# Filler products taken out of a four-layer fused transformer kernel

## The chip, the cores and the metric

The kernel runs on one core of one Trainium2 chip. The metric is the device time of one execution in microseconds (us), lower is better; where several executions of one program are shown, the median stands for them.

The core has four engines with a queue of their own: PE (TensorE, matrix products), DVE (VectorE), ACT (ScalarE) and POOL (GpSimd). SP issues transfers. The profile also prints the clock that PE was granted: 1.00 is its upper level of 2.4 GHz, 0.50 its lower one of 1.2 GHz.

## The reference

Eight sublayers work one after the other on `x` (2048 tokens of 128 numbers) with a context of the same shape. Each takes the layer norm of `x` and adds its gated output to `x`. Cut to what matters:

```python
x = x + tanh(g_xattn[0]) * _L0_xattn_ref(_layernorm(x), ctx, ctx)
x = x + tanh(g_ffn[0])   * _L0_ffn_ref(_layernorm(x), ...)        # turn 0: 16 experts, top 2, and a shared one
x = x + tanh(g_xattn[1]) * _L1_xattn_ref(_layernorm(x), ctx, ...) # turn 1: 16 heads
x = x + tanh(g_ffn[1])   * _L1_ffn_ref(_layernorm(x), ...)        # turn 2: 8 experts, normed twice
x = x + tanh(g_xattn[2]) * _L2_xattn_ref(_layernorm(x), ctx, ctx, mask, ...)  # turn 3
x = x + tanh(g_ffn[2])   * _L2_ffn_ref(_layernorm(x), ...)        # turn 4: 4 experts, top 2
x = x + tanh(g_xattn[3]) * _L3_xattn_ref(ctx, _layernorm(x), ...) # turn 5
x = x + tanh(g_ffn[3])   * _L3_ffn_ref(_layernorm(x), ...)        # turns 6 and 7: attention, then 8 experts

def _L1_ffn_ref(x, Wr, br, W1, b1, g1, be1, W2, b2, g2, be2):
    p = softmax(xt @ Wr + br); probs, idx = top_k(p, 2); probs = probs / probs.sum(-1)
    h = _layernorm(relu(einsum('td,edf->etf', xt, W1) + b1), g1, be1)
    y = _layernorm(relu(einsum('etf,efd->etd', h, W2) + b2), g2, be2)
    return einsum('te,etd->td', gate, y)
```

## The kernel before

The 2048 tokens are worked through in four passes (`for i in range(BLOCKS)`) of 512 tokens, each held as four tiles of 128 tokens. All weights stay on the chip. A pass goes through eight stages in a fixed order; a stage turns its normed rows (tokens by features) into columns with products against the unit matrix, and the code numbers these places 0 to 7: "turn 2" starts the doubly normed experts (`ffn1`), turn 3 the masked attention behind it (`attention` with `k_x2`), turn 4 the four experts `ffn2`, turn 7 the eight experts `ffn3`. Everything is written out by hand: the order on each engine is the order of the code, the four passes are unrolled, and semaphores connect the engines. All data are f32, and a product of 128x512 shows in the profile as two MATMUL records with a weight load (PEld) before each.

At a turn PE has to wait: the last rows of the stage before must be added to `x` (DVE), normed (`layer_norm`, DVE with a root taken by POOL, `give_root`, L251) and then turned (`turn_pairs`, L342, or `turn_pair`, L348) in two pairs of tiles; ACT copies the turned pair to `xnT` (L358, L353), and the first products of the stage follow.

The function `keep_clock` (L331) issues n products of the unit matrix with a weight matrix into bank 1. Nobody reads them. In each pass there are 12:

- in the tail of `ffn1`, two behind the transposes of the combination table (L1045, the call is at L1047), ahead of the wait for ACT's copy of that table, and two behind the product with that table (L1050, the call at L1052), ahead of the wait for the last expert's rows `y` (DVE L1171 to L1177), which the last product L1054 adds;
- by `FILL_BEFORE_ROWS` two at turn 3 (before L348), three at turn 4 and three at turn 7 (before L342), each ahead of the wait for the normed rows `rows_ready`.

After L1054, DVE adds the sum to `x` (L1201) and norms it for turn 3. There, PE computes the queries (L534), the mask products (L479) and the scores (L487). At turn 4 the router products (L1234) let DVE choose the experts (L1301 to L1313), and the products L1243 with the relus L1283 on ACT follow. At turn 7 it is the router L1784, then the products L1792 with the gelus L1850.

```python
FILL_BEFORE_ROWS = (0, 0, 0, 2, 3, 0, 0, 3)
```

Of the kernel before, what the change touches and what calls it, by code (L numbers as in the profile page):

```python
# [34 lines left out]
L3F = dict(wr=8, n1=D, n2=D, w1=8 * 256, w2=16 * D)  # L35


FILL_BEFORE_ROWS = (0, 0, 0, 2, 3, 0, 0, 3)


def width(pieces):
    return sum(pieces.values())
# [63 lines left out]
def wait_for(engine, signal):  # L106
    sem, value = signal
    engine.wait_ge(sem, value)
# [31 lines left out]
def build(nc, args, out):  # L140
    ctx = ExitStack()
    with ctx:
        def sb(name, shape, dt=F32):
            return ctx.enter_context(nc.sbuf_tensor(name, shape, dt))
# [5 lines left out]
        w_x1 = sb("w_x1", [P, width(XA) + width(XB)])  # L150
# [47 lines left out]
        banks = [ctx.enter_context(nc.psum_tensor(f"bank{i}", [P, 512], F32)) for i in range(8)]  # L198
# [10 lines left out]
        ident = k_const["ident"]  # L209
# [70 lines left out]
        def pair_tiles(pair):  # L280
            return (2 * pair, 2 * pair + 1)
# [42 lines left out]
            link(dve.scalar_tensor_tensor(x[:, :, :], rows, tg[:, 7:8], x[:, :, :], ALU.mult, ALU.add))  # L324
            dve.sem_inc(rows_ready, 2)

        def keep_clock(pe, bank, n):


            for _ in range(n):  # L330
                pe.matmul(bank[:, :], ident, w_x1[:, 0:512], start=True, stop=True)  # L331

        def turn_pairs(pe, prev, turn, rows):

            if prev is not None:
                wait_for(pe, prev.bank0)
            for pair in range(2):
                if pair == 0:
                    keep_clock(pe, banks[1], FILL_BEFORE_ROWS[turn])
                pe.wait_ge(rows_ready, 2 * turn + pair + 1)  # L340
                for t in pair_tiles(pair):
                    m = pe.transpose(banks[pair][:, (t % 2) * P:(t % 2 + 1) * P], rows[:, t, :], ident)  # L342
                m.then_inc(rows_turned, 1)

        def turn_pair(pe, turn, rows, pair, bank):
            pe.wait_ge(rows_ready, 2 * turn + pair + 1)
            for t in pair_tiles(pair):
                m = pe.transpose(bank[:, (t % 2) * P:(t % 2 + 1) * P], rows[:, t, :], ident)  # L348
            m.then_inc(rows_turned, 1)
# [99 lines left out]
        def attention(prev, turn_no, after, w, kv, kv_waits, q_bias, neg, finish):  # L449
# [14 lines left out]
            def body(block, q_done, q_ready, scored,  # L464
# [8 lines left out]
                def _(pe):  # L473
# [62 lines left out]
                    if not here:  # L536
                        for signal in kv_waits:
                            wait_for(pe, signal)
                    wait_for(pe, prev.bank0)
                    keep_clock(pe, banks[1], FILL_BEFORE_ROWS[turn_no])  # L540
                    turn_pair(pe, turn_no, xn, 0, banks[0])
                    if kv is kv1:
                        pe.wait_ge(weights_loaded, 16 * 4)
# [238 lines left out]
        def ffn0(i, prev, turn_no, after):  # L782
# [15 lines left out]
            def body(block, rest_cleared, routed, halves_ready, sig_ready, comb_ready, up_done, sil_ready, weighted, hid_ready,  # L798
# [4 lines left out]
                @block.tensor  # L803
                def _(pe):
                    turn_pairs(pe, prev, turn_no, xn_next)
                    pe.wait_ge(l0_loaded, 16)
                    pe.wait_ge(rowsT_ready, 2 * turn_no + 2)
# [151 lines left out]
        def ffn1(prev, turn_no, after):  # L959
# [19 lines left out]
            def body(block, x_done, routed, half_ready, sig_ready, up_done, hT_ready, squares_summed, squared, down_done,  # L979
                     first_variance, first_root, y_raw, second_variance, second_root, y_ready, added, coef_ready,  # L980
                     combT_done, combT_ready, last_done):
                def z_of(e, t):
                    return banks[4 + 2 * (e % 2) + t // 2][:, (t % 2) * 130:(t % 2) * 130 + 130]

                @block.tensor
                def _(pe):
                    kv2.keys(pe, banks[2])
                    kv2.values(pe, 0, banks[4])
                    kv2.values(pe, 1, banks[5])
                    turn_pairs(pe, prev, turn_no, xn)  # L990
                    wait_for(pe, prev.all_used)
                    pe.wait_ge(rowsT_ready, 2 * turn_no + 2)
                    for t in range(TILES):
                        m = pe.matmul(banks[3][:, t * 8:(t + 1) * 8], xnT[:, t * P:(t + 1) * P], k_f1["wr"],
                                      start=True, stop=True)
                    m.then_inc(routed, 1)

                    def up(e):
                        for c in range(4):
                            n = 4 * e + c  # L1000
                            if n >= 3:
                                pe.wait_ge(hT_ready, n - 2)
                            if n == 2:
                                pe.wait_ge(kv2.k_ready, 1)
                            pe.matmul(banks[n % 3][:, :], k_f1["w1"][:, e * 512 + c * P:e * 512 + (c + 1) * P], xnT[:, :],  # L1005
                                      start=True, stop=True).then_inc(up_done, 1)

                    def down(e):
                        pe.wait_ge(hT_ready, 4 * e + 4)
                        if e >= 2:  # L1010
                            pe.wait_ge(y_raw, e - 1)
                        if e == 0:
                            pe.wait_ge(kv2.v_ready, TILES)
                        for t in range(TILES):
                            for c in range(4):
                                pe.matmul(z_of(e, t)[:, 0:129], hT[e % 2][:, c, t * P:(t + 1) * P], w_f1d[:, c, e, :],  # L1016
                                          start=(c == 0), stop=(c == 3))

                    def sum_squares(e):
                        pe.wait_ge(squares_summed, e + 1)  # L1020
                        for t in range(TILES):
                            m = pe.matmul(z_of(e, t)[:, 129:130], sq[e % 2][:, 0, t * P:(t + 1) * P], ones[:, 0:1],
                                          start=True, stop=True)
                        m.then_inc(down_done, 1)

                    def add(e):
                        pe.wait_ge(y_ready, e + 1)
                        if e == 0:
                            pe.wait_ge(half_ready, 1)
                        pe.matmul(banks[3][:, :], ident, y[e % 2].rearrange("p t d -> p (t d)"), start=(e == 0),  # L1030
                                  stop=False).then_inc(added, 1)

                    up(0)
                    for e in range(EXPERTS):
                        if e + 1 < EXPERTS:
                            up(e + 1)
                        down(e)
                        sum_squares(e)
                        if e >= 1:
                            add(e - 1)  # L1040

                    pe.wait_ge(hT_ready, 4 * EXPERTS)
                    pe.wait_ge(coef_ready, 1)
                    for t in range(TILES):
                        m = pe.transpose(banks[0][0:16, t * P:(t + 1) * P], stack[:, t, :], ident)  # L1045
                    m.then_inc(combT_done, 1)
                    keep_clock(pe, banks[1], 2)  # L1047
                    pe.wait_ge(combT_ready, 1)
                    for t in range(TILES):
                        pe.matmul(banks[3][:, t * D:(t + 1) * D], combT[:, t * P:(t + 1) * P], w_f1b[:, :],  # L1050
                                  start=False, stop=False)
                    keep_clock(pe, banks[1], 2)  # L1052
                    pe.wait_ge(y_ready, EXPERTS)
                    pe.matmul(banks[3][:, :], ident, y[(EXPERTS - 1) % 2].rearrange("p t d -> p (t d)"), start=False,  # L1054
                              stop=True).then_inc(last_done, 1)
# [158 lines left out]
        def ffn2(prev, turn_no, after):  # L1214
# [11 lines left out]
            def body(block, routed, shifted, exp_ready, comb_ready, up_done, r_ready,  # L1226
                     sum_ready, turned, gT_ready, down_done, taken):
                @block.tensor
                def _(pe):
                    turn_pairs(pe, prev, turn_no, xn)  # L1230
                    wait_for(pe, prev.all_used)
                    pe.wait_ge(rowsT_ready, 2 * turn_no + 2)
# [936 lines left out]
```

## Time and profile before

| | us |
|---|---|
| median of 3 executions (1696.64 to 1699.97) | 1697.77 |
| the profiled execution | 1694.08 |
| its span, first to last instruction | 1692.3 |
| PE busy in it | 1421.5 (84%) |
| DVE busy | 1087.9 (64%) |
| ACT busy | 736.3 (44%) |
| POOL busy | 410.0 (24%) |
| mean granted clock of PE | 0.939 |

The profile is one execution. Every row of a timeline says when a run of equal instructions began, how long it took, on which engine and line, and in brackets how long the engine had been idle before it and what ended the wait. A row over a stretch of time gives the busy time of each engine in it and the clock that PE was granted there.

### The profile page before, as it was taken

How to read it: one execution, taken by the hardware profiler on the slowest of the kernel's cores; microseconds unless marked ns; L12 is line 12 of the kernel's file. 1: busy time of each engine (PE TensorE's matmuls, PEld its weight loads, DVE VectorE, ACT ScalarE, POOL GpSimd, SP SyncE). 2: the span in 40 equal slices, each digit the busy share in tenths (PEclk: the TensorE clock that was granted, in tenths of full speed). 3: DMA queues.
4: the chain of work that ended last, by engine and by line, in shares of the span. 5: the costliest groups of instructions: out<-in, count | busy, mean ns of one | idle time of the engine just before them, and what ended most of it. 6: DMA issues, size and time to landing. Idle time of an engine off the chain costs nothing. (4 is left out here: it accounts for less than half of the span.)

```text
span 1692.3 us, 28855 instructions
## 1 busy us (share of the span) xinstructions
PE 1421.5 (84%) x11038; PEld 930.3 (55%) x11038; DVE 1087.9 (64%) x3306; ACT 736.3 (44%) x1397; POOL 410.0 (24%) x318
## 2 busy tenths in 40 slices
PE   5788988897877988798878898879887799888977
PEld 4455744564654664366555564446555467445645
DVE  3456765777636676686754676667664667657776
ACT  0254434663334533565424543456432444345632
POOL 1121310630031230261013031055012223116300
PEclk8799999998989999999989999999898999999989
DMA  9000000000000000000000000000000000000000
GB/s 337 0 1 1 1 1 1 1 2 16 1 7 1 1 1 1 1 2 17 1 7 1 1 1 1 1 1 2 16 1 8 1 1 1 1 0 2 2 16 7
DMA packets 16824, 19.60 MB, mean 12 GB/s; under 512 B 3352, under 2 KB 15400, under 8 KB 16172
## 3 DMA queue, kind: packets, MB, share of 16 engines
q1 hardware_dynamic: 16688, 17.75, 3.1%
q8 instruction: 89, 1.46, 0.3%
q14 instruction: 47, 0.39, 0.1%
HBM read 16.70 MB, written 1.05 MB: 10 GB/s over the span
## 5 line engine op out<-in xcount | busy, mean ns | idle before, releaser
L251 POOL TENSOR_TENSOR root<-variance,minus_half 128x2 f32<-128x2 f32 (+1 forms) x75 | 58.2, 776 | 734.1 <-DVE variance L268 460.7
L1068 ACT ACTIVATE work<-bank,w_f 128x512 f32<-128x512 f32 x128 | 88.0, 687 | 118.4 <-PE bank L1005 118.1
L1016 PEld LDWEIGHTS bank<-w_f1d,work 128*128 128x128 f32 x1024 | 119.4, 192 | 15.3 <-issue 15.3
L1571 ACT ACTIVATE work<-work,small 128x128 f32<-128x128 f32 x256 | 78.3, 388 | 96.5 <-DVE small L1703 96.5
L1005 PE MATMUL bank<-xnT,w_f 128*128 128x512 f32 x256 | 119.8, 615 | 0.0
L1016 PE MATMUL bank<-w_f1d,work 128*128 128x129 f32 x1024 | 119.5, 275 | 0.0
L1626 POOL TENSOR_TENSOR small<-small 128x16 f32<-128x16 f32 x32 | 92.9, 2904 | 84.7 <-DVE small L1662 83.1
L1661 DVE TENSOR_REDUCE small<-work 128x16 f32<-128x1024 f32 x48 | 58.5, 1218 | 54.3 <-ACT work L1540 42.9
L1402 PE MATMUL bank<-w_x,cxT 128*128 128x512 f32 x128 | 66.5, 643 | 32.0 <-DVE work L1675 27.1
L1097 POOL TENSOR_TENSOR small<-small,minus_half 128x4 f32<-128x4 f32 x32 | 57.6, 1799 | 139.5 <-DVE small L1136 139.5
L620 DVE TENSOR_REDUCE small<-bank 128x8 f32<-128x512 f32 x96 | 65.6, 683 | 34.6 <-PE bank L487 34.6
L1407 PEld LDWEIGHTS bank<-consts,work 128*128 128x128 f32 x576 | 67.0, 145 | 31.3 <-issue 19.0
L1005 PEld LDWEIGHTS bank<-xnT,w_f 128*128 128x128 f32 x256 | 49.8, 197 | 60.7 <-issue 60.7
L1407 PE MATMUL bank<-consts,work 128*128 128x128 f32 x576 | 77.3, 281 | 5.2 <-DVE work L1675 2.2
L358 ACT COPY xnT<-bank 128x256 f32<-128x256 f32 x32 | 10.9, 374 | 156.1 <-PE bank L342 155.9
L933 DVE TENSOR_TENSOR work<-bank,work 128x256 f32<-128x256 f32 x64 | 27.2, 425 | 80.2 <-POOL work L897 77.5
L502 PE MATMUL bank<-consts,work 128*128 128x128 f32 x384 | 57.5, 286 | 23.6 <-ACT work L586 23.1
L502 PEld LDWEIGHTS bank<-consts,work 128*128 128x128 f32 x384 | 41.5, 143 | 64.4 <-ACT work L586 38.0
L820 PE MATMUL bank<-w_l,xnT 128*128 128x512 f32 x128 | 73.8, 668 | 0.0
L846 PEld LDWEIGHTS bank<-w_l,work 128*128 128x128 f32 x352 | 51.4, 194 | 38.3 <-ACT work L878 31.4
L593 ACT COPY work<-bank 128x512 f32<-128x512 f32 x96 | 53.0, 585 | 43.1 <-PE bank L502 43.1
L586 ACT ACTIVATE work<-work 128x512 f32<-128x512 f32 x96 | 59.3, 631 | 23.3 <-DVE work L621 23.2
(289 smaller groups left out, 3319.2 us busy)
## 6 DMA issues: line engine op xcount, KB each, us to landing
w_f<-in_f_dram SPq DMA_DIRECT2D x1, 2616.0 KB
w_f<-in_f_dram SPq DMA_DIRECT2D x1, 2180.0 KB, 26.6
w_x<-in_x_dram SPq DMA_DIRECT2D x1, 2115.0 KB
w_l<-in_l_dram SPq DMA_DIRECT2D x1, 2088.5 KB, 21.3
w_f1d<-in_f1d_dram SPq DMA_DIRECT2D x4, 512.0 KB
work<-in_x_dram SPq DMA_DIRECT2D x5, 256.0 KB, 2.8
work<-in_ctx_dram SPq DMA_DIRECT2D x5, 256.0 KB, 3.3
out_dram<-x SPq DMA_DIRECT2D x4, 256.0 KB, 2.3
```

What stands on the lines that cost most here:

```text
L502: m = pe.transpose(banks[4 + half][:, (c % 4) * P:(c % 4 + 1) * P], p_sb[t % 2][:, c * P:(c + 1) * P], ident)
L586: act.activation(p_sb[t % 2][:, own], s_sb[t % 2][:, own], ACT.Exp).then_inc(p_ready, 1)
L620: link(dve.tensor_reduce(mx[:, t, hs], s, AX, ALU.max))
L820: m = pe.matmul(a[:, :], xt, k_l0["gu"][:, g * 512:(g + 1) * 512], start=True, stop=True)
L1005: pe.matmul(banks[n % 3][:, :], k_f1["w1"][:, e * 512 + c * P:e * 512 + (c + 1) * P], xnT[:, :], start=True, stop=True).then_inc(up_done, 1)
L1016: pe.matmul(z_of(e, t)[:, 0:129], hT[e % 2][:, c, t * P:(t + 1) * P], w_f1d[:, c, e, :], start=(c == 0), stop=(c == 3))
L1068: act.activation(hT[e % 2][:, c, :], banks[n % 3][:, :], ACT.Relu, bias=k_f1["b1"][:, n:n + 1]).then_inc(hT_ready, 1)
L1402: pe.matmul(banks[j][:, :], cxT[:, b, :, :], half_of(k_x3["wkv"], j), start=True, stop=True).then_inc(k_done, 1)
L1407: m = pe.transpose(bank[:, (c % 4) * P:(c % 4 + 1) * P], rows[:, c * P:(c + 1) * P], ident)
L1571: ins = act.activation(s_sb[b % 2][:, c * P:(c + 1) * P], s_sb[b % 2][:, c * P:(c + 1) * P], ACT.Exp, bias=negmax[b % 2][:, c:c + 1])
L1626: pool.tensor_tensor(k_rs, k_ssq, half_power, ALU.pow).then_inc(k_rooted, 1)
L1661: link(dve.tensor_reduce(dst, sq.rearrange("p (h d) -> p h d", d=XD), AX, ALU.add))
```

## The change

All calls of `keep_clock`, the function and the table `FILL_BEFORE_ROWS` go. Nothing else is edited. The waits stay; where a filler product stood first behind a wait, the next instruction of PE carries it.

```diff
-FILL_BEFORE_ROWS = (0, 0, 0, 2, 3, 0, 0, 3)
...
-        def keep_clock(pe, bank, n):
-            for _ in range(n):
-                pe.matmul(bank[:, :], ident, w_x1[:, 0:512], start=True, stop=True)
-
         def turn_pairs(pe, prev, turn, rows):
             if prev is not None:
                 wait_for(pe, prev.bank0)
             for pair in range(2):
-                if pair == 0:
-                    keep_clock(pe, banks[1], FILL_BEFORE_ROWS[turn])
                 pe.wait_ge(rows_ready, 2 * turn + pair + 1)
...
                     wait_for(pe, prev.bank0)
-                    keep_clock(pe, banks[1], FILL_BEFORE_ROWS[turn_no])
                     turn_pair(pe, turn_no, xn, 0, banks[0])
...
                     m.then_inc(combT_done, 1)
-                    keep_clock(pe, banks[1], 2)
                     pe.wait_ge(combT_ready, 1)
...
-                    keep_clock(pe, banks[1], 2)
                     pe.wait_ge(y_ready, EXPERTS)
```

The line numbers of the changed kernel are lower by 9 to 12 (L348 is L339 there, L1054 is L1042, L342 is L333). PE's order of one pass at the end of `ffn1` and the start of turn 3, before (`y` is in `work`; L1045 turns the combination table, L1050 uses it, L1054 is the last product, L348 turns the first rows of turn 3, L534 are the queries):

```order
232 L1045 MATMUL bank<-consts,small 16x128 [waits coef_9,hT_9]
233 L1045 MATMUL bank<-consts,small 16x128 x3
234 L331 MATMUL bank<-w_x,consts 128x512 x2
235 L1050 MATMUL bank<-w_f1b,small 128x128 [waits combTr_9]
236 L1050 MATMUL bank<-w_f1b,small 128x128 x3
237 L331 MATMUL bank<-w_x,consts 128x512 x2
238 L1054 MATMUL bank<-work,consts 128x512 [waits y_ready_9]
239 L331 MATMUL bank<-w_x,consts 128x512 [waits combTr_9,v_ready_3,k_ready_3]
240 L331 MATMUL bank<-w_x,consts 128x512
241 L348 MATMUL bank<-consts,xn 128x128 [waits rows_ready_1]
242 L348 MATMUL bank<-consts,xn 128x128
243 L534 MATMUL bank<-xnT,w_x 128x256 [waits rowsT_ready_1]
```

The same place on PE after the change:

```order
232 L1035 MATMUL bank<-consts,small 16x128 [waits coef_9,hT_9]
233 L1035 MATMUL bank<-consts,small 16x128 x3
234 L1039 MATMUL bank<-w_f1b,small 128x128 [waits combTr_9]
235 L1039 MATMUL bank<-w_f1b,small 128x128 x3
236 L1042 MATMUL bank<-work,consts 128x512 [waits y_ready_9]
237 L339 MATMUL bank<-consts,xn 128x128 [waits combTr_9,rows_ready_1,v_ready_3,k_ready_3]
238 L339 MATMUL bank<-consts,xn 128x128
239 L525 MATMUL bank<-xnT,w_x 128x256 [waits rowsT_ready_1]
```

Six products are gone, and three more waits stand at the first turned tile. At turn 7, PE before (L528 is the last projection of the attention, L1784 the router, L1792 the first experts' products):

```order
550 L528 MATMUL bank<-w_a,small 128x128 [waits oT_ready_13]
551 L331 MATMUL bank<-w_x,consts 128x512 [waits s_ready_13]
552 L331 MATMUL bank<-w_x,consts 128x512 x2
553 L342 MATMUL bank<-consts,xn 128x128 [waits rows_ready_1]
554 L342 MATMUL bank<-consts,xn 128x128
555 L342 MATMUL bank<-consts,xn 128x128 [waits rows_ready_1]
556 L342 MATMUL bank<-consts,xn 128x128
557 L1784 MATMUL bank<-w_f,xnT 128x8 [waits rowsT_ready_1,taken_13]
558 L1784 MATMUL bank<-w_f,xnT 128x8 x3
559 L1792 MATMUL bank<-xnT,w_f 128x512 x2
```

And after:

```order
544 L519 MATMUL bank<-w_a,small 128x128 [waits oT_ready_13]
545 L333 MATMUL bank<-consts,xn 128x128 [waits rows_ready_1,s_ready_13]
546 L333 MATMUL bank<-consts,xn 128x128
547 L333 MATMUL bank<-consts,xn 128x128 [waits rows_ready_1]
548 L333 MATMUL bank<-consts,xn 128x128
549 L1772 MATMUL bank<-w_f,xnT 128x8 [waits rowsT_ready_1,taken_13]
550 L1772 MATMUL bank<-w_f,xnT 128x8 x3
551 L1780 MATMUL bank<-xnT,w_f 128x512 x2
```

The three products between the projection and the first turned tile are gone; turn 4 looks the same. No instruction moves on DVE, ACT, POOL or SP.

## Rows read from the trace of the kernel before

**Rows 1.** The page's busy line (engine, us, share, count), and the records of L331.

```profile
PE 1421.5 (84%) x11038; PEld 930.3 (55%) x11038; DVE 1087.9 (64%) x3306; ACT 736.3 (44%) x1397; POOL 410.0 (24%) x318
...
L331 PE MATMUL bank<-w_x,consts x96: 592/712/1062, 217.7 to 1645.2; 128*128 128x512 f32 x96
```

**Rows 2.** Timeline, first pass, tail of `ffn1`: start, us, engine, line, operation, out<-in.

```profile
215.02 2.07 PE L1030 MATMUL bank<-work,consts 128*128 128x512 f32 x2 [1.26 <-DVE work L1164]
...
221.55 0.87 DVE L1177 TENSOR_SCALAR work<-work,small 128x128 f32<-128x128 f32 x4
222.34 1.98 PE L331 MATMUL bank<-w_x,consts 128*128 128x512 f32 x4
...
224.16 1.02 PE L1054 MATMUL bank<-work,consts 128*128 128x512 f32 x2
...
225.22 0.48 DVE L1201 SCALAR_TENSOR_TENSOR x<-bank,tg,x 128x256 f32<-128x256 f32 x1 [2.80 <-PE bank L1054]
```

**Rows 3.** Timeline, third pass, the same place.

```profile
1038.85 0.48 DVE L1201 SCALAR_TENSOR_TENSOR x<-bank,tg,x 128x256 f32<-128x256 f32 x1 [1.22 <-PE bank L1054]
```

**Rows 4.** Stretches from:to, length, busy us (count) of PE, PEld, DVE, ACT, POOL, clock, DMA share, GB/s.

```profile
214.40:221.10 6.70, 6.08 (x10) 2.25 (x10) 5.24 (x26) 4.93 (x9) 1.90 (x2) 0.50 0.00 0
...
255.40:262.10 6.70, 6.12 (x10) 2.92 (x11) 3.20 (x14) 0.00 (x0) 0.70 (x1) 0.50 0.00 0
...
419.20:422.50 3.30, 3.30 (x6) 1.48 (x6) 2.21 (x11) 0.00 (x0) 0.99 (x2) 0.50 0.00 0
422.60:426.00 3.40, 2.85 (x16) 1.87 (x15) 1.02 (x2) 0.85 (x3) 0.61 (x1) 1.00 0.00 0
466.95:477.15 10.20, 6.57 (x16) 3.59 (x16) 4.01 (x27) 2.17 (x4) 0.15 (x1) 0.50 0.10 26
```

**Rows 5.** The same view: turn 3 to turn 4, second and third pass.

```profile
635.36:663.16 27.80, 23.47 (x288) 12.82 (x289) 18.19 (x36) 10.41 (x20) 1.39 (x2) 0.97 0.01 2
1042.39:1071.90 29.51, 25.18 (x289) 13.28 (x289) 18.20 (x36) 10.41 (x20) 1.39 (x2) 0.93 0.01 2
```

**Rows 6.** Groups by line: the mask products in these, third pass, then second pass.

```profile
L479 PE MATMUL bank<-neg,consts 128*128 128x512 f32 x16 | 9.3, 711 | 0.0
```

```profile
L479 PE MATMUL bank<-neg,consts 128*128 128x512 f32 x16 | 7.6, 599 | 0.0
```

**Rows 7.** Timeline, first pass, turn 4.

```profile
256.57 5.33 PE L331 MATMUL bank<-w_x,consts 128*128 128x512 f32 x6
...
259.01 0.60 DVE L276 TENSOR_SCALAR xn<-x,norm_small,root 128x128 f32<-128x128 f32 x2 [0.81 <-POOL root L251]
...
263.11 1.03 PE L1234 MATMUL bank<-w_f,xnT 128*128 128x4 f32 x8 [0.61 <-ACT xnT L358]
...
264.25 0.17 DVE L1301 TENSOR_TENSOR small<-bank,w_f 128x16 f32<-128x16 f32 x1 [4.38 <-PE bank L1234]
...
268.14 3.67 PE L1243 MATMUL bank<-w_f2e,xnT 128*128 128x512 f32 x8 [0.46 <-ACT work L1283]
```

**Rows 8.** Timeline, third pass, turn 4.

```profile
1071.90 4.03 PE L331 MATMUL bank<-w_x,consts 128*128 128x512 f32 x6
```

**Rows 9.** Timeline, first pass, turn 7.

```profile
419.33 4.34 PE L331 MATMUL bank<-w_x,consts 128*128 128x512 f32 x6
...
422.24 1.38 DVE L307 SCALAR_TENSOR_TENSOR xn<-xn,root,w_f 128x128 f32<-128x128 f32 x2 [0.81 <-POOL root L251]
...
423.51 0.66 PE L342 MATMUL bank<-consts,xn 128*128 128x128 f32 x4
...
425.61 1.96 PE L1792 MATMUL bank<-xnT,w_f 128*128 128x512 f32 x4
...
427.95 3.80 PE L1792 MATMUL bank<-xnT,w_f 128*128 128x512 f32 x8 [0.38 <-ACT work L1850]
```

**Rows 10.** Timeline, second pass, turn 0, which has no fillers.

```profile
471.27 1.86 PE L809 MATMUL bank<-w_l,xnT 128*128 128x17 f32 x8 [0.55 <-ACT xnT L358]
472.97 3.76 PE L820 MATMUL bank<-w_l,xnT 128*128 128x512 f32 x4
```

## The prediction

> **What bounds the kernel now.** I read the busy line first. PE is busy 84% of the span, DVE 64%, ACT 44% [rows 1]: no other engine is near PE, so what PE does at half speed costs time wherever its work is dense. Then the records of L331: 12 products in each of four passes, two records each, 96 in all [rows 1]. A record takes about 0.43 us at the upper clock (four in 1.98 us, [rows 2]) and 0.89 us at the lower one (six in 5.33 us, [rows 7]). Nobody reads their results, so they can matter in two ways alone: they hold PE when real work is ready, and they work on the clock. Last, the granted clock by stretches [rows 4], which shows the second. In the first pass it is low from before the first filler of the `ffn1` tail, since PE had waited there, and full once the fillers have run. It is low again at turn 4 and at turn 7 after PE's waits, and at turn 0, where no filler stands.
>
> **What a low clock costs.** The third pass gives the price. Its stage from turn 3 to turn 4 has one stretch at the low clock more than that of the second pass (mean 0.93 against 0.97) and takes 29.51 us against 27.80 us, 1.71 us more [rows 5]. The mask products L479, the same 16 records, take 9.3 us against 7.6 us, and so hold all of it [rows 6]: what PE loses at a turn comes out at the stage's end unshortened. PE at half speed loses half of the time that it works at the low clock.
>
> **How long it lasts without fillers.** The next question is how much dense work PE does before the clock is back. The rows give four cases. At turn 4 the first pass starts its fillers at 256.57 us and is still low at 262.10 us: 5.5 us [rows 4, 7]. The third pass there runs six records in 4.03 us; at 0.89 us low and 0.43 us high that is about 3.1 slow ones, 2.8 us [rows 8]. At turn 7 it is from 419.33 to some time after 422.50 us, 3.2 us [rows 4, 9]. At turn 0, without fillers, the products start at 472.97 us and the clock is still low at 477.15 us: 4.2 us [rows 4, 10]. The transposes and the eight narrow router records ahead of them at turn 0 did not bring it back. So I take about 4 us of dense work at the low clock, between 2.8 and 5.5 us, counted from the first dense product of the stage, and half of that as loss.
>
> **Tail of `ffn1` (four products).** In the first pass `y` is ready at 221.55 + 0.87 = 222.42 us, but L1054 begins at 224.16 us, behind fillers [rows 2]. The cover ends 1.74 us late. It then takes 1.02 us at the full clock. Without fillers L1054 starts at about 222.5 us, but the clock has been low since before they ran, and such a product then takes 2.07 us (L1030, [rows 2]). DVE gets it at about 224.6 instead of 225.22 us: 0.6 us sooner. In the third pass the fillers end in time and DVE waits just 1.22 us [rows 3]; there the slow product costs 1.0 us. The other two passes I put between these ends, at a gain of 0.2 us. Sum over four passes: 0.0 us, with -2.4 and +4.0 us (all as the one or the other) as its ends. The other two fillers stand before L1050, whose result the same L1054 adds; it is done before `y` either way. The three waits of the first filler of turn 3 move to L348, where nothing else is queued.
>
> **Turn 3 (two products).** They run while DVE norms, and hold nobody. In passes 1, 2 and 4 the clock is full behind them. Without them PE comes to L348 at the low clock. Queries and mask products are dense from there on: 4 us at half speed cost 2.0 us, and the slower transposes 0.1 us. In the third pass the low stretch is there already at 1.71 us [rows 5, 6], so just 0.4 us is added. Sum: 3 x 2.1 + 0.4 = 6.7 us.
>
> **Turn 4 (three products).** Here fillers stand in the way. The second pair of rows is normed at 259.01 + 0.60 = 259.61 us, the fillers end at 261.90 us, and the router starts at 263.11 us [rows 7]. Without fillers transposes, copy and router wait for that pair alone: about 0.6 us of transposes and 0.6 us of copy and wakening later the router starts at about 260.9 us, 2.2 us sooner. It takes 1.86 us instead of 1.03 us (turn 0's at the low clock, [rows 10]; it is not wider than that), so DVE chooses 1.4 us sooner. The first four products L1243 follow at 262.7 us. All at the low clock they would take 6.8 us; with 4 us low, 4 + (4 - 4/1.71) x 0.86 = 5.4 us, so the next four start at 268.1 us, where they start now (268.14 us, [rows 7]). The gain and the loss cancel: 0.0 us, between -0.7 and +1.3 us. In the third pass the fillers were 1.3 us shorter [rows 7, 8]; the gain is smaller by about that much: +1.2 us. Sum: 0.1 x 3 + 1.2 = 1.5 us.
>
> **Turn 7 (three products).** Here they cost nothing now: the second pair is ready at 422.24 + 1.38 = 423.62 us, and PE turns the first at 423.51 us [rows 9]. By then the clock is back [rows 4]. Without them it is low: the router takes 0.8 us longer [rows 4, 10], transposes 0.1 us. The products L1792 then start at about 426.6 us. Two at the low clock take 3.5 us, so the third starts at 430.1 instead of 427.95 us, and what is left of the low clock costs another 0.3 us: 2.5 us, of which the 0.38 us that PE waits there now for ACT is already taken off. The ends are 1.7 us (clock back after 2.8 us) and 3.2 us (after 5.5 us and more). The stage behind it keeps PE dense, so I carry it whole. Sum: 4 x 2.4 = 9.6 us.
>
> **The sum.** 0.0 + 6.7 + 1.5 + 9.6 = 17.8 us. The profiled execution took 1694.08 us (span 1692.3 us) and would take 1711.9 us. The median of the runs is 3.7 us above it; 1697.77 + 17.8 = 1715.6 us, and I say 1715 us, 1.0% slower.
>
> **Rivals.**
>
> *The fillers are mere load* (faster). If the clock comes back without them as soon as with them, only their place on the path counts: 1.7 us in the first tail, 0.0 in the third, between these in the others, some 4.5 us in all; 2.2 us at turn 4 in three passes and 0.9 us in one, 7.5 us. The time is 1697.8 - 12 = 1686 us. For it speaks that at turns 4 and 7 most of the fillers run at the low clock themselves [rows 7, 9]. Against it speaks turn 0, where the clock stayed low for 4.2 us of real products, and the third pass, where one low stretch cost 1.71 us. It decides if less than about 1.2 us of dense work runs at the low clock after each turn. The Trainium skill (TensorE: Matmul & The Clock Gate, section "What's actually happening") says that for modeling, the ramp penalty is under 1% of a typical kernel's span. By that rule this rival would be right. The trace does not bear it out: a mean clock of 0.939 means that 12% of the span ran at the low level. Chance 0.08.
>
> *Slack takes it.* At turn 3 and turn 7 the loss on PE is taken up by waits for DVE and ACT further on, and the small gains at turn 4 remain. The time stays within 3.4 us of 1697.8 us. The third pass speaks against it for turn 3 [rows 5]; for turn 7 the rows show no second case. Chance 0.07.
>
> *The clock stays low longer.* Sparse work at the start of the stages (transposes, waits for copies) delays its return to the 5.5 us of dense work that turn 4 shows. Then turn 3 costs 2.8 x 3 + 1.1 = 9.5 us, turn 4 about 1.3 x 3 + 2.5 = 6.4 us, turn 7 about 3.2 x 4 = 12.8 us, 29 us in all: 1726 us. Chance 0.20.
>
> *The change does not do what it says*: the order on PE has all 48 products fewer, and no compiler pass put others there. I leave it out.
>
> **How the numbers follow.** My forecast has 0.65, the long low clock 0.20, slack 0.07, the faster case 0.08. A measurement of this kernel can tell about 0.2%, 3.4 us, from no change. Slower by more than that: 0.65 + 0.20 = 0.85, less 0.01 for the low end of my own case, 0.84. Within: 0.08. Faster: 0.08. The range goes from 1704 us (the tail at its gain, turn 7 at 1.7 us and turn 3 at 1.4 us a pass) to 1725 us (nearly all of the long case). Where the low stretches fall differs from pass to pass in the trace, so each term will scatter by its bounds, and the sum by less.
>
> **What would show it.** In the changed kernel the clock should be 0.50 from before the last product of `ffn1` into the mask products of turn 3 in every pass, and again over the first products of turns 4 and 7. The stage from turn 3 to turn 4 should take 29.5 to 30.5 us in all four passes instead of 27.8 us in three. DVE should get the last product of `ffn1` 2.2 us after `y` is ready. The router of turn 4 should start 1.3 us behind the normed rows. From the normed rows of turn 7 to the third experts' product it should take 6.5 us instead of 4.3 us. The mean granted clock should fall to about 0.91. I am wrong if the clock is full within 1 us of the first dense products, if the stage from turn 3 stays at 27.8 us, or if other stages gain or lose low stretches because all work shifts in time.

## The result and the profile after

The changed kernel takes 1717.67 us (median of 4 runs, 1716.92 to 1719.14) against 1697.2 us (median of 4 runs of the kernel before, 1692.7 to 1699.97). The ratio of the two kernels, estimated from all these runs, is 1.0124, with a 95% interval of 1.0101 to 1.0148: 1.2% slower. The profiled execution took 1716.92 us.

The head of its page, which answers to [rows 1]:

```profile
span 1715.1 us, 28675 instructions
...
PE 1401.0 (82%) x10942; PEld 923.2 (54%) x10942; DVE 1085.3 (63%) x3306; ACT 739.3 (43%) x1397; POOL 409.6 (24%) x318
```

The 96 records of L331 are gone. PE is busy 20.5 us less, and the span is 22.8 us longer. (That is more than the 20.5 us between the medians, because the profiled execution of the kernel before, at 1694.08 us, was 3.1 us faster than the median.) The mean granted clock fell from 0.939 to 0.915.

First pass, tail of `ffn1` and turn 3 (timeline; L1165, L1042 and L1189 are the old L1177, L1054 and L1201, L339 the old L348). It answers to [rows 2]:

```profile
222.34 0.88 DVE L1165 TENSOR_SCALAR work<-work,small 128x128 f32<-128x128 f32 x4
223.27 2.08 PE L1042 MATMUL bank<-work,consts 128*128 128x512 f32 x2 [1.03 <-DVE work L1165]
225.38 0.48 DVE L1189 SCALAR_TENSOR_TENSOR x<-bank,tg,x 128x256 f32<-128x256 f32 x1 [2.17 <-PE bank L1042]
...
229.01 0.66 PE L339 MATMUL bank<-consts,xn 128*128 128x128 f32 x2 [3.67 <-DVEq L290]
230.14 1.22 PE L525 MATMUL bank<-xnT,w_x 128*128 128x256 f32 x2 [0.46 <-ACT xnT L344]
231.15 3.62 PE L470 MATMUL bank<-neg,consts 128*128 128x512 f32 x4
```

The last product now starts 0.05 us after `y` is ready (222.34 + 0.88 = 223.22 us), takes 2.08 us, and DVE gets it 2.2 us behind `y`. The first four records of the mask products take 3.62 us, twice what they take at the upper clock.

The granted clock (stretches as in [rows 4]: PE, PEld, DVE, ACT, POOL busy, clock), first pass, and for turn 0 of the second:

```profile
215.25:235.55 20.30, 13.15 (x28) 5.75 (x32) 10.17 (x46) 5.62 (x11) 3.43 (x4) 0.50 0.00 1
235.70:238.90 3.20, 2.74 (x16) 1.26 (x8) 2.53 (x4) 1.27 (x3) 0.00 (x0) 1.00 0.00 0
262.95:269.70 6.75, 6.20 (x15) 3.72 (x16) 2.71 (x23) 1.22 (x4) 0.00 (x0) 0.50 0.00 1
...
426.85:433.50 6.65, 5.21 (x14) 3.25 (x15) 2.94 (x21) 2.45 (x4) 0.37 (x1) 0.50 0.00 0
433.70:437.00 3.30, 3.30 (x8) 1.08 (x7) 2.81 (x17) 1.99 (x4) 0.00 (x0) 1.00 0.01 2
471.30:488.10 16.80, 9.73 (x25) 5.73 (x26) 6.64 (x33) 3.65 (x8) 1.60 (x4) 0.50 0.06 16
```

Before, the clock was low from 214.4 to 221.1 us at this place; now it is low for over 20 us in one piece, up to 235.55 us, well into turn 3.

First pass, turn 4 (L275, L1222, L1289, L1231 are the old L276, L1234, L1301, L1243), against [rows 7]:

```profile
262.14 0.60 DVE L275 TENSOR_SCALAR xn<-x,norm_small,root 128x128 f32<-128x128 f32 x2 [0.81 <-POOL root L250]
264.07 1.84 PE L1222 MATMUL bank<-w_f,xnT 128*128 128x4 f32 x8 [0.55 <-ACT xnT L349]
265.77 9.09 PE L1231 MATMUL bank<-w_f2e,xnT 128*128 128x512 f32 x16
266.02 0.17 DVE L1289 TENSOR_TENSOR small<-bank,w_f 128x16 f32<-128x16 f32 x1 [3.01 <-PE bank L1222]
```

From the normed rows to DVE's first step it was 264.25 - 259.61 = 4.64 us [rows 7]; it is 266.02 - 262.74 = 3.28 us. That is the gain of 1.4 us. The first eight and the second eight records together were done at 271.81 us before (268.14 + 3.67, [rows 7]), and are done at 274.86 us now: from the normed rows 12.2 and 12.1 us. The gain is gone.

First pass, turn 7 (L306, L1772, L1780, L1865 are the old L307, L1784, L1792, L1877), against [rows 9]:

```profile
426.24 1.39 DVE L306 SCALAR_TENSOR_TENSOR xn<-xn,root,w_f 128x128 f32<-128x128 f32 x2 [0.81 <-POOL root L250]
427.74 0.69 PE L333 MATMUL bank<-consts,xn 128*128 128x128 f32 x2 [3.73 <-DVEq L308]
428.98 1.85 PE L1772 MATMUL bank<-w_f,xnT 128*128 128x8 f32 x8 [0.55 <-ACT xnT L349]
430.68 7.03 PE L1780 MATMUL bank<-xnT,w_f 128*128 128x512 f32 x12
439.44 0.19 DVE L1865 TENSOR_SCALAR small<-bank 128x32 f32<-128x32 f32 x1 [1.75 <-PE bank L1788]
```

The same step of DVE in the trace before:

```profile
433.47 0.19 DVE L1877 TENSOR_SCALAR small<-bank 128x32 f32<-128x32 f32 x1 [0.87 <-PE bank L1800]
```

From the normed rows to this step it was 433.47 - 423.62 = 9.85 us and is 439.44 - 427.63 = 11.81 us: 2.0 us lost.

**Where the 22.8 us are.** DVE runs the same instructions in the same order in both kernels. For each, I took its start in the trace after less its start in the trace before. The table shows by how much this difference grew from one mark to the next: `y` of the last expert ready, first L1201 (ends "tail"), rows normed for turn 4 (ends "turn 3"), first group of turn 5, behind the expert sums L1328 (ends "turn 4"), rows for turn 6, rows for turn 7, first experts added at turn 7 (L1887). "Turns 0 to 2" of a pass are what lies ahead of its own `y`. In us:

| pass | tail | turn 3 | turn 4 | turn 5 | turn 6 | turn 7 | turns 0 to 2 |
|---|---|---|---|---|---|---|---|
| 1 | -0.62 | +2.98 | -0.10 | +1.07 | -0.11 | +1.97 | -0.02 |
| 2 | -0.22 | +2.84 | +0.12 | +1.02 | -0.21 | +1.90 | +1.10 |
| 3 | +0.95 | +0.98 | +1.32 | -0.44 | -0.57 | +1.88 | -0.33 |
| 4 | -0.25 | +2.85 | +0.12 | +1.05 | -0.16 | +1.91 | +1.05 |
| sum | -0.14 | +9.65 | +1.46 | +2.70 | -1.05 | +7.66 | +1.80 |

The preparation ahead of the first pass adds 0.8 us. The four places of the change hold 18.6 us (-0.14 + 9.65 + 1.46 + 7.66), the others 4.2 us.

Of the signs that the prediction named, these came: the clock was low in one piece from before the last product of `ffn1` into turn 3 in all four passes, the router of turn 4 began 1.3 us behind the normed rows (264.07 - 262.74), and the mean clock is 0.915. The third experts' product of turn 7 began 6.2 to 6.3 us behind the normed rows (forecast 6.5, before 4.3), and turn 3 took 30.5 to 30.6 us from its first turned tile to PE's last product, a little over the 29.5 to 30.5 us of the forecast.

### The profile page after: what moved, and what is told of

Read it like the earlier page. It is cut to its first block and busy times, and to the rows that moved or that the text cites. A ratio compares the mean times of both kernels' runs of the same rounds, so it can differ in the third digit from the quotient of the medians.

```text
span 1715.1 us, 28675 instructions
## 1 busy us (share of the span) xinstructions
PE 1401.0 (82%) x10942; PEld 923.2 (54%) x10942; DVE 1085.3 (63%) x3306; ACT 739.3 (43%) x1397; POOL 409.6 (24%) x318
## 3 DMA queue, kind: packets, MB, share of 16 engines
HBM read 16.70 MB, written 1.05 MB: 10 GB/s over the span
## 5 line engine op out<-in xcount | busy, mean ns | idle before, releaser
L611 DVE TENSOR_TENSOR work<-bank,small 128x512 f32<-128x512 f32 x96 | 66.4, 692 | 3.3
```

The source lines that it names most:

```text
L611: ins = dve.tensor_tensor(d, s, mx[:, t, hs].unsqueeze(2).to_broadcast([P, 8, SEQ]), ALU.subtract)
```

## The experiments

The theory: a filler product is worth what it brings back of the clock, and what a place loses without it is half of the dense work that PE then does at the low clock. The rival: the fillers are load, and cost just what they hold up. Every run is compared with runs of the kernel before on the same chip. Changes per stage are read as in the table above, against the first trace of the kernel before. Each kernel has one trace (the kernel before has two), and a single stage can move by 1.7 us with no edit at all, as the second trace of the kernel before shows further down; so ratios are firmer than the changes of one stage.

**One group at a time.** Turn 7 alone:

```diff
-FILL_BEFORE_ROWS = (0, 0, 0, 2, 3, 0, 0, 3)
+FILL_BEFORE_ROWS = (0, 0, 0, 2, 3, 0, 0, 0)
```

> Only the three filler products at turn 7 are gone. Theory (the loss is work at the low clock): the clock is low over the router and the first two experts' products, and each pass loses 1.9 us between the normed rows and the third product, as in the changed kernel; 7.7 us over four passes, ratio about 1.0045. Rival (the fillers are mere load): they hid under a wait at turn 7, so the time does not change, ratio 1.000. What else moves is the place of other low stretches: within 3 us either way.

Measured: ratio 1.0056 (1.0038 to 1.0075). Turn 7 lost 3.4, 3.5, 1.9 and 3.5 us. The rival is out here: nothing was held up, and removing work cost 12.2 us in the trace. The price is that of the changed kernel in one pass of four, and nearly twice that in three. The stretch of its first pass:

```profile
420.25:433.85 13.60, 9.56 (x21) 4.94 (x22) 8.27 (x48) 3.94 (x7) 1.71 (x2) 0.50 0.00 1
```

In the same trace the dense products behind that turn:

```profile
427.83 8.50 PE L1792 MATMUL bank<-xnT,w_f 128*128 128x512 f32 x12
```

The clock came back 6.0 us after these products began (427.83 to after 433.85 us). In the changed kernel it was 2.9 us (430.68 to after 433.50 us), and the same 12 records took 8.50 us instead of 7.03 us. The same edit at the same place costs 1.9 or 3.5 us, by how long the low stretch lasts.

Turn 4 alone:

```diff
-FILL_BEFORE_ROWS = (0, 0, 0, 2, 3, 0, 0, 3)
+FILL_BEFORE_ROWS = (0, 0, 0, 2, 0, 0, 0, 3)
```

> Only the three filler products at turn 4 are gone. Theory: DVE chooses 1.2 to 1.4 us sooner, and the products at the low clock take it back; per pass 0.0, 0.0, 1.3 and 0.0 us, in all 1.4 us or ratio 1.001. Rival (mere load): the 2.2 us that they stand in the way are gained in three passes and 0.9 us in one, 7.5 us faster, ratio 0.9955.

Measured: ratio 1.0049 (1.0030 to 1.0068), more than the theory said and on the other side of the rival. Turn 4 lost 0.8, 1.2, 0.9 and 1.3 us, 4.2 us in all, where the changed kernel lost 1.5 us. Its first pass:

```profile
254.70:268.20 13.50, 9.44 (x21) 5.31 (x22) 7.04 (x37) 2.46 (x6) 0.84 (x2) 0.50 0.00 1
```

```profile
262.46 9.98 PE L1243 MATMUL bank<-w_f2e,xnT 128*128 128x512 f32 x16
```

The products ran at the low clock for 5.7 us (262.46 to after 268.20), 4.0 us in the changed kernel (265.77 to between 269.70 and 269.90 us). The medians are 7.5 us apart, so turn 4 explains about half. In the same trace turn 5 is 3.8 us longer (+1.5 us in three passes), but the second trace of the kernel before has 2.7 us there with no edit; where the other half of the 0.49% lies is not shown.

Turn 3 alone:

```diff
-FILL_BEFORE_ROWS = (0, 0, 0, 2, 3, 0, 0, 3)
+FILL_BEFORE_ROWS = (0, 0, 0, 0, 3, 0, 0, 3)
```

> Only the two filler products at turn 3 are gone, the four of the ffn1 tail stay. Theory: the clock is full at the last product of the tail, PE then waits 3.5 us instead of 1.9 us, and in passes that did not have it before a low stretch follows in the mask products, at 1.7 us each; passes 1, 2 and 4 take 29.5 instead of 27.8 us from turn 3 to turn 4, the third stays; 5 us or ratio 1.003. Rival (mere load): no change, ratio 1.000.

Measured: ratio 1.0046 (1.0028 to 1.0065). Turn 3 lost 2.6, 2.5, 0.8 and 2.6 us, 8.5 us where I expected 5 us, and turn 4 gained 3.7 us of it back, because its low stretch was shorter. First pass:

```profile
222.00:228.60 6.60, 3.92 (x15) 2.02 (x14) 3.39 (x15) 0.00 (x0) 0.72 (x2) 1.00 0.00 0
228.80:235.40 6.60, 5.34 (x12) 2.25 (x16) 1.37 (x5) 0.76 (x2) 0.69 (x1) 0.50 0.01 2
```

The tail's fillers had brought the clock to full. PE then waited 3.67 us for the rows, and the clock fell before the first turned tile. So the two products at turn 3 bridge a wait.

The tail alone:

```diff
                     m.then_inc(combT_done, 1)
-                    keep_clock(pe, banks[1], 2)
                     pe.wait_ge(combT_ready, 1)
...
-                    keep_clock(pe, banks[1], 2)
                     pe.wait_ge(y_ready, EXPERTS)
```

> Only the four filler products in the ffn1 tail are gone, the two at turn 3 stay. Theory: DVE gets the last product 0.6 us sooner in the first pass, 0.2 us in the second and fourth, 0.95 us later in the third; the two fillers of turn 3 then run at the low clock, 3.5 us long, and just fill the wait, so that the clock comes back at the first products of turn 3 or one low stretch later: 0 to 1.7 us per pass, in all about 3 us or ratio 1.002. Rival (mere load): 4.5 us faster, ratio 0.997.

Measured: ratio 0.9984 (0.9970 to 0.9998), faster. My theory was on the wrong side here, and the ratio of the rival (0.997) lies at the edge of the interval. The hand-over (L1201's start behind `y`) moved as expected, by -0.63, -0.22, +0.95 and -0.25 us, though, and not by the 4.5 us of the rival. What I had not expected is turn 3: no pass lost there, and the third gained 1.5 us. Its first pass:

```profile
217.00:227.00 10.00, 7.31 (x18) 3.69 (x17) 6.18 (x29) 3.94 (x7) 2.05 (x2) 0.50 0.00 0
227.20:233.90 6.70, 4.92 (x19) 1.66 (x17) 2.93 (x14) 0.76 (x2) 1.40 (x2) 1.00 0.01 2
```

```profile
224.09 2.08 PE L1054 MATMUL bank<-work,consts 128*128 128x512 f32 x2 [1.03 <-DVE work L1177]
225.96 2.47 PE L331 MATMUL bank<-w_x,consts 128*128 128x512 f32 x4
229.75 0.44 PE L348 MATMUL bank<-consts,xn 128*128 128x128 f32 x2 [1.32 <-DVEq L291]
```

L1054 at the low clock and the fillers behind it are dense work of their own. The clock came back at about 227.1 us, while they ran, and it was full when the rows came. The two fillers of turn 3 do the job by themselves. The four of the tail do not pay.

The other traces bear this out better than this one alone. Four of them are of kernels without the tail fillers and with those of turn 3 (this one and three below); in all their 16 passes the stage from the first L1201 to the rows of turn 4 was within 0.3 us of the shortest. In the four traces that have both groups (two of the kernel before, turn 4 alone and turn 7 alone) 5 of 16 passes were 1.7 us longer.

**Tail and turn 3 together**, both edits above:

> The four fillers of the ffn1 tail and the two of turn 3 are gone, those of turns 4 and 7 stay. Theory (the clock returns only after a few us of dense work, whoever does it): as in the changed kernel the clock is low from before the last product of the tail into turn 3, and turn 3 costs 2.9 us a pass in three passes and 1.0 us in one, 9.6 us, less what a low stretch at turn 4 is then spared (1.2 us a pass in the kernel without the turn 3 fillers alone): 6 to 10 us, ratio about 1.005. Rival (the two groups add up as measured alone: +0.46% and -0.16%): ratio 1.003.

Measured: ratio 1.0062 (1.0045 to 1.0079). The sum of the two alone would be 1.003, which lies below the interval; but that sum has an interval of about 0.2% itself, so the medians decide little. With the second measurement of the tail, further down (0.9966), the sum would be 1.001, and the gap is clear. Turn 3 lost 3.0, 2.5, 1.3 and 2.6 us, 9.5 us, as in the changed kernel. The first pass was low through to turn 3:

```profile
222.00:235.40 13.40, 8.24 (x18) 2.94 (x18) 4.82 (x21) 0.76 (x2) 1.39 (x2) 0.50 0.00 1
```

Without the turn 3 fillers, taking out the tail's no longer gains (1.0062 against 1.0046 for turn 3 alone); that it costs is not shown, since these two intervals overlap. Turn 4, which keeps its fillers here, gained 2.3 us.

**The same program twice.** The kernel before, unchanged:

> The kernel before, unchanged, for a second trace. Theory: the small terms that no removed filler explains (about 1 us a pass from turn 5 to turn 6, 1 us at turns 0 to 2) come from where low stretches fall, which differs from execution to execution; so two traces of the same program differ by single stretches of low clock and by 0.7 to 1.7 us at each, 1 to 5 us in all. Rival: these terms belong to the change; then two traces of the same program agree within 0.3 us in every stage.

Measured: 1698.57 us; the span of this trace is 1696.8 us. The same code differs from its first trace by -1.7 to +1.8 us in single stages, and by +1.4, +1.3, -1.4 and +1.5 us at turn 5 (2.7 us in sum). A place at turn 5 of the first pass, first in this trace, then in the first one:

```profile
311.35:318.05 6.70, 6.12 (x16) 3.95 (x17) 4.49 (x7) 2.37 (x4) 6.55 (x3) 0.50 0.00 0
```

```profile
311.00:313.20 2.20, 0.90 (x2) 0.48 (x3) 2.17 (x5) 0.23 (x1) 1.47 (x1) 1.00 0.00 0
313.40:316.65 3.25, 3.25 (x12) 2.12 (x11) 2.03 (x4) 1.78 (x3) 3.11 (x3) 0.50 0.00 0
```

The low stretch is twice as long. The +2.7 us at turn 5 in the table of the changed kernel is therefore no effect that a removed product must explain: the same program shows the same 2.7 us there. The rival, agreement within 0.3 us in every stage, is out. The stages of the change move as well: the tail by -1.6, +0.3, +0.8 and -1.0 us (-1.4 us in sum) and turn 3 by +1.7, 0.0, -1.7 and +1.7 us (+1.6 us).

**Three tries at a faster kernel, and the tail once more.** Two fillers instead of three at turn 4, with the tail ones gone (the tail's edit as above):

```diff
-FILL_BEFORE_ROWS = (0, 0, 0, 2, 3, 0, 0, 3)
+FILL_BEFORE_ROWS = (0, 0, 0, 2, 2, 0, 0, 3)
```

> The kernel without the four tail fillers, and with two instead of three at turn 4; two at turn 3 and three at turn 7 stay. Theory: at turn 4 two fillers at the low clock end 1.7 us sooner, at about 0.7 us behind the normed rows instead of 2.3 us, and DVE chooses up to 1.6 us sooner; if the clock still comes back as early, the gain is up to 1.6 us a pass, 0.3% under the kernel without the tail ones; if it comes back later, the products lose the same or more, up to 1.7 us a pass. I expect ratio 0.998, between 0.995 and 1.002. Rival (mere load): 0.9955.

Measured: ratio 1.0000 (0.9987 to 1.0013). In the trace turn 4 moved by -2.2, -2.2, +0.7 and +1.6 us, so it was shorter where the clock came back as early and longer where it did not. The 0.998 that I expected lies outside the interval. Over all it does not beat the kernel with three.

Eight new fillers behind `ffn3`, in PE's longest wait, with the tail ones gone:

```diff
                         if s == EXPERTS + 1:
                             turn_normed_context(pe)
+                    keep_clock(pe, banks[1], 8)
```

> The kernel without the four tail fillers, and with eight new ones behind the last expert of ffn3, where PE waits 7.75 us for the end of the pass and the clock is low for 10 us of turn 0. Theory: the clock stays full through turn 0; transposes and router are 1.2 us sooner in each of passes 2 to 4, and what DVE and ACT do next hides the rest; 3 to 4 us faster than without them, ratio 0.996. Rival (mere load): nothing gained, ratio as without the tail ones, 0.998.

Measured: ratio 0.9999 (0.9989 to 1.0009). There is no gain, though the theory expected one (0.996); the rival's 0.998 lies outside the interval too, so the eight fillers cost about what taking out those of the tail gains. Turn 0 of the second pass:

```profile
462.50:476.30 13.80, 8.94 (x29) 4.08 (x27) 6.70 (x40) 2.40 (x5) 1.16 (x2) 1.00 0.07 19
476.45:483.10 6.65, 5.33 (x13) 3.27 (x14) 1.27 (x3) 1.37 (x4) 1.79 (x3) 0.50 0.00 0
```

```profile
469.64 0.66 PE L342 MATMUL bank<-consts,xn_next 128*128 128x128 f32 x4 [1.70 <-DVEq L907]
477.77 0.69 PE L833 MATMUL bank<-consts,work 128*128 128x128 f32 x2 [4.01 <-DVE work L933]
478.24 1.92 PE L820 MATMUL bank<-w_l,xnT 128*128 128x512 f32 x2
```

The clock stayed full over the transposes, the router and the first products, as meant. But these were then done so early that PE waited 4.01 us for DVE's choice of experts (2.23 us in the kernel before and after at the same place), and the clock fell there. The low stretch was moved, and it was shorter (6.7 us against 10.2 us in [rows 4]), but turns 0 to 2 were 1.8 us longer than in the first trace of the kernel before. The fourth pass did the same (a wait of 4.02 us). In the third the fillers did not even hold the clock: it was low over the router and all that followed,

```profile
879.30:892.70 13.40, 11.18 (x28) 6.50 (x29) 4.75 (x28) 3.66 (x8) 1.79 (x3) 0.50 0.00 1
```

and turns 0 to 2 were 1.7 us longer there.

Only the second two of the tail gone, those right ahead of L1054:

```diff
-                    keep_clock(pe, banks[1], 2)
                     pe.wait_ge(y_ready, EXPERTS)
```

> Only the second two fillers of the ffn1 tail are gone, those right ahead of its last product; the first two stay, and those of turns 3, 4 and 7. Theory: the first two run in a wait and bring the clock back by 221.2 us of the first pass, so the last product starts at once when y is ready and at the full clock: 1.7 us sooner in the first pass, 1.3 in the second and fourth, 0 in the third; the wait ahead of turn 3 stays as long as before. 4 us faster, ratio 0.997 to 0.998. Rival (the clock needs the second two as well): the last product is slow in some passes and turn 3 starts at the low clock in some, ratio 1.000 or above.

Measured: ratio 0.9990 (0.9976 to 1.0005). The hand-over moved by -1.6, -1.2, 0.0 and -1.2 us, 4.0 us in all, as expected, but the ratio is not the 0.997 to 0.998 that the theory gave, and its interval holds 1. Turn 3 was 1.7 and 1.6 us longer in the first two passes, and 1.7 us shorter in the third:

```profile
219.40:229.50 10.10, 6.11 (x21) 2.66 (x19) 7.41 (x34) 1.75 (x4) 2.31 (x3) 1.00 0.00 0
229.70:233.00 3.30, 3.30 (x5) 1.69 (x6) 0.56 (x2) 0.38 (x1) 0.00 (x0) 0.50 0.02 5
```

With the clock at full the two fillers of turn 3 are over in 1.88 us and PE waits 1.86 us behind them. At the low clock they take up to twice as long and fill the wait, as in the kernel without any in the tail. That this is why turn 3 gave time back is argued, not shown: the second trace of the kernel before has the same first pass with all four fillers in the tail (hand-over -1.6 us, turn 3 +1.7 us),

```profile
229.45:232.75 3.30, 3.30 (x6) 1.50 (x5) 0.49 (x2) 0.38 (x1) 0.00 (x0) 0.50 0.03 5
```

and the third and fourth pass here had the same early hand-over and no low stretch behind it.

And that kernel once more, beside the last one on the same chip:

> The kernel without the four tail fillers once more, beside the one that keeps the first two of them. Theory: 0.998 again, the interval clear of 1; and slower than or equal to the kernel that keeps the first two, which has the same hand-over or a better one. Rival (the first measurement was the place of low stretches): 1.000.

Measured: ratio 0.9966 (0.9953 to 0.9979). Both measurements lie clear of 1, at 0.2% and 0.3%. It beats both kernels: the one before by these, the changed one by 1.4 to 1.6% (1.0124 divided by 0.9984 or 0.9966). The second half of what I expected failed: this kernel is not slower than or equal to the one that keeps the first two tail fillers, but faster, 1692.4 us against 1697.81 us on the same chip, although its hand-over comes later.

## Why the prediction was right, and where it was off

The forecast was 1715 us, 17.8 us above the median of before, and the measured time is 1717.67 us, 20.5 us above the median measured beside it. The mechanism is shown: three of the four groups alone each made the kernel slower, one of them (turn 7) with nothing held up that could have been gained. The rival of mere load, 1686 us, is out. For the tail alone it came nearer than my theory did (0.997 against 1.002, measured 0.9984 and 0.9966). The ratios of the four groups alone add up to 1.35%, inside the interval of the change (1.01% to 1.48%).

**Price of the low clock.** Half of the dense work at it: this held. That 12% of the span ran at the low level was not yet a price, as I used it against the mere-load rival: half speed costs at most half of that, and only where nothing hides it; turn 7 alone decides against the rival. The 0.43 us for a record at the upper clock was too low for the rows that I gave: four in 1.98 us are 0.50 us each, and from start to start it is 0.46 us ((224.16 - 222.34) / 4, [rows 2]); the lower bound of 2.8 us that I worked out with it becomes 2.7 us. At turn 7 the 12 records took 7.03 or 8.50 us with 2.9 or 6.0 us of low clock, 1.5 us for 3.1 us.

**How long it lasts.** Here the step was right on the mean and wrong by place. I took 4 us for all, between 2.8 and 5.5 us. It was 5.4 us at turn 3 (230.14 to after 235.55 us), 4.0 at turn 4, and 2.9 at turn 7 in the first pass of the changed kernel, and within 0.6 us of that in its other passes; with turn 7 alone edited it was 6.0 us, outside my bound.

**Tail.** 0.0 us forecast, -0.1 us measured, pass by pass as worked out (-0.6, between, +1.0, between). This is measured against the first trace of the kernel before, from which the term was worked out; against the second it would be +1.3 us, and turn 3 8.0 us instead of 9.65 us. The two together are 9.5 or 9.3 us, whichever trace one takes.

**Turn 3.** 6.7 us forecast, 9.65 us measured. The term was mis-sized by that duration: 2.9 us a pass instead of 2.1 us, 1.0 instead of 0.4 us in the third. The long-low-clock rival had 9.5 us here.

**Turn 4.** 1.5 us forecast, 1.5 us measured. DVE chose 1.4 us sooner, and the products took it back. The edit alone measured 4.2 us in its trace, so that the agreement owes something to where the clock came back.

**Turn 7.** 9.6 us forecast, 7.7 us measured. The router took 1.85 us as said; the clock came back after 2.9 us of products, not 4. Alone, the same edit lost 12.2 us. The forecast lies between.

**Luck.** The four terms sum to 18.6 us in the traces against the 17.8 us forecast, but turn 3 is 3.0 us over and turn 7 1.9 us under. That the sum agrees so closely is partly these two cancelling. The low end of the range was also added up wrongly: the terms named for it, -2.4 + 4 x 1.7 + 3 x 1.4 = 8.6 us, give 1706 us, not 1704 us.

**What I had put at nothing.** Stages without fillers moved by 4.2 us in sum. I had named this as a way to be wrong and not priced it. The second trace of the kernel before moved by 4.1 us in the same stages with no edit.

**The tail as an edit of its own.** My sum treated tail and turn 3 as separate terms. They depend on each other: where turn 3 keeps its fillers, taking out the tail's gained in both measurements, and where turn 3 has none it did not (1.0062 against 1.0046). For this change, which removes both, the sum did not suffer.

**Open.** Why turn 4 alone costs 4.2 us and with the others 1.5 us in the traces is told by where the clock came back, and that was seen in one trace of each kernel; the medians do not separate it. The same holds for turn 7, 12.2 us alone and 7.7 us with the others. The ratios of tail and turn 3 together, turn 4 and turn 7 add up to 1.67%, more than the 1.24% of the change, so the groups may cost less together than apart; the runs were on different chips, and this was not tested. Whether fillers at another place of turn 0, in the wait for the choice of experts, gain what the eight behind `ffn3` did not was not tried.

## What to carry to other kernels

A product that nobody reads can pay where PE waits and then meets dense work: price it as half of the dense time at the low clock against what it delays. Here the fillers in the last wait before the dense work paid (turns 3, 4 and 7), and those further up, with another wait behind them, did not (the tail, the eight behind `ffn3`). Whether a longer filling of the wait at turn 3 would pay was not tried. Remove and add such groups one at a time and also together, since the worth of one can depend on the next.

## What the runs showed of the hardware

- The low clock lasted between 2.9 and 6.0 us of dense products after a wait, for the same code at the same place (turn 7).
- Eight router records of 128x8, back to back for 1.85 us, ended with the clock still low (turn 7 of the changed kernel); they took 1.85 us, against 1.03 us at the upper clock in the kernel before.
- The same program, traced twice, had low stretches in different places, and single stages differed by up to 1.8 us; 22 runs of it on one chip went from 1689.53 to 1699.74 us. One trace of each kernel can't settle a difference of that size.
- With the clock up over turn 0 (eight fillers behind `ffn3`, second pass), PE came early to its next wait, which grew from 2.23 to 4.01 us, and the clock fell in that one.
